# Last stage of a two-layer block on one core, written out step by step instead of looped

## The chip, the cores and the metric
The kernel runs on one core of a Trainium2 chip, as one program from the first load to the last store. The metric is its device time in microseconds (us): 528.04 us before the change (median of 3 runs, 527.6 to 529.25). Engines are called by the profile's names: PE is the matrix engine (PEld its weight loads), DVE the vector engine, ACT the scalar engine, POOL the GpSimd engine, SP the queue that issues most plain DMAs.

## The reference, cut to what matters
x has 8 sequences of 1024 rows of 256 numbers. Two layers follow one another, each adding a product of an attention branch and a gate to x:

```python
xn = _layernorm(x)                       # eps 1e-5
s = _L0_attn_ref(xn, L0_attn_W)          # linear attention
g = _silu(_L0_ffn_ref(xn, gate_w, wg, wu, wd))   # one of 8 experts per row
x = x + s * g
xn = _layernorm(x)
s = _L1_attn_ref(xn, W_qkv, W_out, b_out)        # causal softmax attention in blocks of 128
g = _silu(_L1_ffn_ref(xn, ..., ln_g, ln_b))
x = x + s * g
```

The last feed-forward part sees 8 positions and 16 heads, so each head picks 8 // 16 = 0 rows and adds nothing: what is left of it is a second norm, `(y - mean) * rsqrt(var + eps) * ln_g + ln_b`, over the already normalized rows. The kernel therefore needs two factors per row: 1/sqrt(var + eps) for the attention's input, and the scale of the norm of the normalized row for the gate.

## The kernel before, in words
The program has three stages. The first normalizes the rows, does the linear attention's sums and sorts the rows by expert in DRAM. The second runs the experts on sorted tiles and writes their rows to DRAM (`expert_rows`). The third, `second_layer`, is the one that changes. It handles 64 tiles of 128 rows as 32 units of two tiles; n below is a unit's number.

Each engine has a function `step(n, ...)` and runs it for n in order, so the work is a software pipeline: step n of an engine handles different parts of units near n. The order of every queue is written by hand:
- POOL, step n: `rows_free(n+8)` waits until the indices are there and the buffer is free; `norm_scale(n+2)` makes the row factors with two small operations, `rstd` (L1901, a power of -0.5) and `shift` (L1903); `add_x(n+5)` (L1893) is a DMA that adds x to the unit's rows; `gather(n+8)` (L1883) issues two indirect DMAs that fetch the unit's expert rows. Before `norm_scale` it waits in `rows_scaled(n+5)` for DVE's scaling of that unit's rows.
- DVE, step n: `result(n-2)` (L1809), `index(n+9)` (L1714, converts the next two index columns from float to integer), `norm_stats(n+3)` (L1738), `centre_gate(n+1)` (L1762), `find_moments(n+3)` (L1748), `gate(n-1)` (L1775), `prepare_norm(n+3)` (L1754 to L1756, three operations on two to four numbers per partition), `base_divisor`, `scale_gate(n+1)` (L1769), `maximum(n)` (L1781), `invert_divisor`, `gate_rows(n-1)` (L1803), and last `scale_rows(n+6)` (L1720), which needs the gathered rows.
- ACT, step n: copies of PE's results, `exp(n-1)`, `norm_apply(n+2)` (L1652, writes `xn2nd` and waits for `shift`), `begin_attend`, `tanh(n)`.
- PE, step n: `q(n)` (L1515), `turn(n+1)` (L1528, transposes `xn2nd` and waits for it), `v(n)` (L1537), `turn_probs(n-1)` (L1547), `scores(n)` (L1557), `attend(n-1)` (L1568).
- SP stores the results (L1492).

The first units have an order of their own. For units 0 to 7 x comes by plain loads and DVE adds it (`sum_x`, L1726) right after `scale_rows`; the pair is called `first_rows`. For units 0 to 3 (`NORMED = SLOTS`) the statistics are found at once (`first_norm`). `first_rows(5)` and `first_rows(6)` stand in DVE's step 0, `first_rows(7)` in step 1. On POOL, the factors of units 0 to 3 come in steps -5 to -2; those of unit 4 come in step 2, behind the gathers of units 7, 8 and 9.

The steps are run by `pipeline`: up to n = 7 and from n = 24 on they are written out by Python, and in between a hardware loop (`Fori`) runs twice over eight steps, n = 8 to 23, with addresses worked out from the loop's register. Stage one has no such loop.

Of the kernel before, what the change touches and what calls it, by code (L numbers as in the profile page):

```python
# [14 lines left out]
P = 128  # L15
# [22 lines left out]
def program(nc, x, W, gate_w, wg, wu, wd, W_qkv, W_out, b_out, ln_g, ln_b, out):  # L38
# [16 lines left out]
    with ExitStack() as whole:  # L55
# [16 lines left out]
        z.zinv = sb("zinv", [P, Q_SLOTS, z.UT])  # L72

        z.four = sb("four", [P, 4, z.UT, z.D])
        z.gather_u = sb("gather_u", [P, 8, z.UT], U32)
# [64 lines left out]
def scope(nc, z, ctx, stage):  # L140
# [12 lines left out]
def pipeline(eng, first, step, last, units, slots, tail=1):  # L153


    for n in range(first, slots):
        step(n, n % slots, n // slots)
    with eng.Fori(1, units // slots - tail) as r:
        for i in range(slots):
            step(r * slots + i, i, r)  # L160
    for n in range(units - tail * slots, last + 1):
        step(n, n % slots, n // slots)


def mm3(nc, out, lhs, rhs, first, last, **kw):
# [45 lines left out]
def first_layer(nc, z, W, gate_w, wg, wu, wd):  # L211
# [13 lines left out]
    with ExitStack() as ctx:  # L225
# [698 lines left out]
        def gpsimd(pool):  # L924
# [57 lines left out]
                                    pattern=[[-1, P]], channel_multiplier=1).then_inc(g["consts"], 1)  # L982
            nc.gpsimd.memset(ones_s, 1.0).then_inc(g["consts"], 1)
            nc.gpsimd.iota(ids[:], pattern=[[1, z.SLOTS]], base=0, channel_multiplier=0).then_inc(g["consts"], 1)
            nc.gpsimd.memset(z.neg_half[:], -0.5)
            nc.gpsimd.memset(z.minus_one[:], -1.0)
            nc.gpsimd.memset(xn[:, :, :, D - 1:D], 1.0)
            for e in range(E):
# [15 lines left out]
def experts(nc, z, W_qkv, W_out, b_out, ln_g, ln_b):  # L1004
# [7 lines left out]
    with ExitStack() as ctx:  # L1012
# [287 lines left out]
        def vector(dve):  # L1300
# [23 lines left out]
            def prepare(part):  # L1324

                if part == 0:
                    nc.vector.tensor_tensor(shift_all[:], z.chosen[:], z.moved[:].unsqueeze(1).to_broadcast([P, z.TILES, E]), ALU.mult).then_inc(g["shifts_ready"], 1)
                if part == 1:
                    dve.wait_ge(g["shifts_ready"], 1)
                    nc.vector.tensor_reduce(shift[:], shift_all[:], AX_X, ALU.add).then_inc(g["shift_found"], 1)  # L1330
                if part == 2:
                    dve.wait_ge(g["shift_found"], 1)
                    nc.vector.tensor_tensor(z.place[:, 0:z.TILES], z.place[:, 0:z.TILES], shift[:], ALU.subtract).then_inc(g["shift_found"], 1)
                    nc.vector.tensor_scalar(z.last_one[:], z.ident[:], z.ident[:, P - 1:P], None, ALU.mult).then_inc(z.set_up, 1)
                if part == 3:
                    dve.wait_ge(g["shift_found"], 2)
                    nc.vector.tensor_copy(z.gather_u[:], z.place[:, 0:8 * z.UT].rearrange("p (n t) -> p n t", t=z.UT)).then_inc(z.index_ready, 8)
                if part in (4, 5, 6):
                    of = slice((part - 4) * D, (part - 3) * D)
                    dve.wait_ge(g["weights_loaded"], 16 * 6)  # L1340
                    nc.vector.tensor_tensor(z.w2[:, :, of], z.w2[:, :, of], w2_end[:, of].unsqueeze(1).to_broadcast([P, KD, D]), ALU.subtract).then_inc(g["w2_centred"], 1)
                if part == 7:
                    nc.vector.tensor_scalar(z.lng_half[:], z.lng[:], 0.5, None, ALU.mult).then_inc(z.set_up, 1)
# [68 lines left out]
def second_layer(nc, z):  # L1412
# [7 lines left out]
    UT = 2  # L1420
    UNITS = z.TILES // UT
    SLOTS, TURN = 4, 8
    DIRECT, NORMED = 2 * SLOTS, SLOTS
    MOE_SPACE = 3648
    assert UNITS % TURN == 0 and UT * D <= 512
    with ExitStack() as ctx:
# [35 lines left out]
        g = sems("moe_scaled x_summed stats_done moments_ready var_ready rstd_ready shift_ready xn_ready t_ready t_copied q_ready q_copied "  # L1462
                 "v_ready v_copied s_ready top_ready p_ready pt_ready pt_copied att_ready z_based z_ready "
                 "z_tanh gate_ready total_based inv_ready gated out_ready "
                 "banks_cleared s_begun a_begun folded_ready folded_copied")
# [11 lines left out]

            return not isinstance(n, int) or least <= n < UNITS

        run = lambda eng, first, step, last: pipeline(eng, first, step, last, UNITS, TURN)  # L1480
        at = lambda i, ahead: (i + ahead) % TURN
        turns = lambda n, i, k: (n - i % SLOTS) * (k // SLOTS)

# [224 lines left out]
            run(act, -1, step, UNITS)  # L1708

        def vector(dve):  # L1710
            def index(n, i):

                if there(n):
                    nc.vector.tensor_copy(gather_u[:, i], z.place[:, bass.ds(UT * n, UT)]).then_inc(z.index_ready, 1)  # L1714

            def scale_rows(n, i):

                if there(n):
# [31 lines left out]
            def prepare_norm(n, i):  # L1750

                if there(n):
                    dve.wait_ge(g["moments_ready"], UT * n + UT)
                    nc.vector.tensor_scalar(neg_mean[:, i % SLOTS], moments[:, i % SLOTS, :, 0], -1.0, None, ALU.mult).then_inc(g["var_ready"], 1)  # L1754
                    nc.vector.tensor_scalar(var_eps[:, i % SLOTS, 0], moments[:, i % SLOTS, :, 1], LN_EPS, None, ALU.add).then_inc(g["var_ready"], 1)
                    nc.vector.tensor_scalar(var_eps[:, i % SLOTS, 1], moments[:, i % SLOTS, :, 1], 1.0 + LN_EPS, LN_EPS * LN_EPS, ALU.mult, ALU.add).then_inc(g["var_ready"], 1)  # L1756

            def centre_gate(n, i):
                if there(n):
                    dve.wait_ge(g["shift_ready"], n + 1)  # L1760
                    for t in range(UT):
                        nc.vector.scalar_tensor_tensor(zg[:, i % SLOTS, t, :].unsqueeze(1), one_tile(n, t), neg_mean[:, i % SLOTS, t:t + 1], z.lng_half[:].unsqueeze(1),  # L1762
                                                       ALU.add, ALU.mult).then_inc(g["z_based"], 1)

            def scale_gate(n, i):
                if there(n):
# [57 lines left out]
            def step(n, i, _):  # L1824
# [26 lines left out]
                if isinstance(n, int) and n + 6 < DIRECT:  # L1851
                    if n != -1:
                        first_rows(n + 6, at(i, 6))
                    if n + 6 < NORMED:
                        first_norm(n + 6, at(i, 6))
                else:
                    scale_rows(n + 6, at(i, 6))

            def divisors(p):
# [12 lines left out]
        def gpsimd(pool):  # L1872
            def rows_free(n, i):

                if there(n):
                    pool.wait_ge(z.index_ready, n + 1)
                    if there(n, SLOTS):
                        pool.wait_ge(g["moe_scaled"], n - SLOTS + 1)

            def gather(n, i):  # L1880
                if there(n):
                    for t in range(UT):
                        nc.gpsimd.indirect_dma_start(  # L1883
                            out=moe[:, i % SLOTS, t, :], out_offset=None, in_=z.expert_dram.ap(),
                            in_offset=bass.IndirectOffsetOnAxis(ap=gather_u[:, i, t:t + 1], axis=0)).then_inc(moe_loaded[i % SLOTS], 16)

            def rows_scaled(n, i):
                if there(n):
# [6 lines left out]
            def norm_scale(n, i):  # L1895
                if there(n):
                    if there(n, SLOTS):

                        pool.wait_ge(g["xn_ready"], n - SLOTS + 1)
                    pool.wait_ge(g["var_ready"], 3 * n + 3)  # L1900
                    nc.gpsimd.tensor_tensor(rstd[:, i % SLOTS], var_eps[:, i % SLOTS], z.neg_half[:, 0:2 * UT].rearrange("p (a t) -> p a t", a=2), ALU.pow).then_inc(g["rstd_ready"], 1)  # L1901
                    pool.wait_ge(g["rstd_ready"], n + 1)
                    nc.gpsimd.tensor_tensor(shift[:, i % SLOTS], neg_mean[:, i % SLOTS], rstd[:, i % SLOTS, 0], ALU.mult).then_inc(g["shift_ready"], 1)  # L1903

            def step(n, i, _):
                first = isinstance(n, int) and n + 5 < NORMED
                normed = not first and isinstance(n, int) and n + 2 < NORMED
                direct = isinstance(n, int) and n + 5 < DIRECT
# [8 lines left out]
                if not direct:  # L1917
                    add_x(n + 5, at(i, 5))
                if not first:
                    gather(n + 8, at(i, 8))  # L1920

            for stored in z.stored:
# [27 lines left out]
```

## Time and profile before

| | us |
|---|---|
| time, median of 3 runs | 528.04 |
| time of the profiled execution | 526.61 |
| its span, first to last instruction | 524.9 |
| PE busy | 502.5 (96%) |
| DVE busy | 459.6 (88%) |
| ACT busy | 391.8 (75%) |
| POOL busy | 315.4 (60%) |

The granted clock of PE is 0.996 of full speed. The 3.1 us between the median and the span are 1.7 us around the span in the profiled execution, and 1.4 us by which that execution lay below the median. The busy shares are averages over three stages: DVE and POOL are much busier in the last 200 us (stage three) than these figures say, and a step of that stage has to be read from the timeline.

### The profile page before, as it was taken

What the parts mean: (1) busy time and instruction counts of PE and PEld (TensorE: products, weight loads), DVE (VectorE), ACT (ScalarE), POOL (GpSimd) and SP (SyncE); (2) the same over time, 40 slices, a digit from 0 to 9 for tenths busy, and PEclk for the clock granted to TensorE, in tenths of its full rate; (3) what the DMA queues carried; (4) which work ended last, traced back from release to release, by engine and by line L of the source; (5) the groups of instructions that cost most, each with busy time, mean ns of one, the idle gap of its engine ahead of it and who ended that gap; (6) DMA issues with size and microseconds to landing.
All of it is one profiled execution on the core that took longest, in us unless ns stands there. A gap on an engine that the chain in (4) does not pass through costs nothing.

```text
span 524.9 us, 12534 instructions
## 1 busy us (share of the span) xinstructions
PE 502.5 (96%) x3576; PEld 463.5 (88%) x3577; DVE 459.6 (88%) x1479; ACT 391.8 (75%) x891; POOL 315.4 (60%) x395
## 2 busy tenths in 40 slices
PE   6899999999999999899999999889999999999995
PEld 5899999999999998788999987779888888888894
DVE  6899999999999978589878848899999999999985
ACT  4878878787778863576777746778878887789883
POOL 5468876767777776222122038788888888786410
PEclk9999999999999999999999999999999999999998
DMA  8942322222331115666777454246555665556311
GB/s 224 239 122 93 110 81 81 81 83 87 97 85 67 51 61 194 168 192 191 248 230 230 148 183 151 68 115 139 133 121 125 134 135 128 135 128 120 74 50 61
DMA packets 59409, 67.74 MB, mean 129 GB/s; under 512 B 11864, under 2 KB 53728, under 8 KB 59360
## 3 DMA queue, kind: packets, MB, share of 16 engines
q1 hardware_dynamic: 44960, 39.34, 25.2%
q0 software_dynamic: 14400, 27.80, 21.6%
q8 instruction: 24, 0.39, 0.3%
q14 instruction: 25, 0.20, 0.1%
HBM read 39.85 MB, written 27.26 MB: 128 GB/s over the span
## 4 chain that ended last, share of the span: by engine, by line
PE 63%; DVE 20%; issue 7%; POOL 3%; DMA 2%; ACT 2%; DVEq 1%; SPq 0%; POOLq 0%; ACTq 0%
PE gu_ps L1117 6%; PE v_ps L1537 4%; PE q_ps L1515 3%; PE k_ps L167 3%; PE t_ps L1093 3%; PE y_ps L1136 3%; PE m_ps L167 3%; DVE zg L1762 3%; PE m_ps L169 3%; PE m_ps L168 3%; PE k_ps L168 3%; PE k_ps L169 3%; PE tq_ps L167 3%; PE tq_ps L168 3%; PE tq_ps L169 3%
## 5 line engine op out<-in xcount | busy, mean ns | idle before, releaser
L1883 POOL DMA_INDIRECT four<-expert_rows,gather_u x64 | 70.0, 1094 | 42.5 <-DMA expert_rows<-y 22.3
L948 POOL DMA_INDIRECT sorted_rows<-xn,row_u x64 | 68.0, 1063 | 17.2 <-issue 14.4
L937 POOL TENSOR_TENSOR xn<-xn 128x512 fp32r<-128x512 f32 x32 | 43.2, 1349 | 30.7 <-ACT xn L562 30.6
L1537 PE MATMUL v_ps<-wvo,xt 128*128 128x256 f32 x256 | 60.6, 380 | 0.0
L1515 PE MATMUL q_ps<-xt,wqk 128*128 128x256 f32 x256 | 60.6, 380 | 0.0
L208 POOL DMA_DIRECT2D four<-sorted_rows x36 | 19.4, 540 | 58.7 <-issue 29.4
L1515 PEld LDWEIGHTS q_ps<-xt,wqk 128*128 128x128 f32 x256 | 48.6, 190 | 6.8 <-issue 0.4
L1652 ACT ACTIVATE xn2nd<-res,shift,rstd 128x256 f32<-128x256 f32 (+1 forms) x64 | 34.9, 593 | 23.3 <-POOL shift L1903 23.1
L1537 PEld LDWEIGHTS v_ps<-wvo,xt 128*128 128x128 f32 x256 | 46.4, 191 | 4.9
L1901 POOL TENSOR_TENSOR rstd<-var_eps,neg_half 128x4 f32<-128x4 f32 x32 | 38.6, 1207 | 15.3 <-DVE var_eps L1756 8.2
L1117 PE MATMUL gu_ps<-wgu,xgt 128*128 x288 | 40.2, 283 | 1.2 <-issue 0.9
L167 PE MATMUL tq_ps<-xt,wq 128*128 128x256 f32 x128 | 38.5, 301 | 1.8 <-DVE xt L696 1.8
L552 ACT ACTIVATE xn<-four,shift,rstd 128x255 f32<-128x255 f32 x64 | 34.9, 600 | 6.0 <-POOL shift L931 6.0
L590 ACT ACTIVATE k<-kf 128x512 fp32r<-128x512 f32 x32 | 20.2, 630 | 24.8 <-DVE kf L709 24.8
L167 PE MATMUL k_ps<-wkg,xt 128*128 128x264 f32 x128 | 37.8, 296 | 0.2 <-DVE logit L710 0.2
L1117 PEld LDWEIGHTS gu_ps<-wgu,xgt 128*128 128x128 f32 x288 | 35.0, 192 | 3.0 <-issue 1.9
L167 PE MATMUL m_ps<-k,xn 128*128 128x256 f32 x128 | 36.3, 284 | 0.4 <-DVE k L715 0.4
L168 PE MATMUL k_ps<-wkg,xt 128*128 128x264 f32 x128 | 36.5, 285 | 0.0
L169 PE MATMUL k_ps<-wkg,xt 128*128 128x264 f32 x128 | 36.4, 284 | 0.0
L169 PE MATMUL m_ps<-k,xn 128*128 128x256 f32 x128 | 36.1, 282 | 0.0
L168 PE MATMUL m_ps<-k,xn 128*128 128x256 f32 x128 | 36.1, 282 | 0.0
L1893 POOL DMA_DIRECT2D res<-in_L_attn_x x24 | 31.9, 1328 | 6.7 <-issue 6.7
(262 smaller groups left out, 1780.8 us busy)
## 6 DMA issues: line engine op xcount, KB each, us to landing
expert_rows<-y SPq DMA_DIRECT2D x36, 256.0 KB, 2.8
four<-in_L_attn_x SPq DMA_DIRECT2D x32, 256.0 KB, 2.9
out_rows<-att SPq DMA_DIRECT2D x32, 256.0 KB, 2.3
res<-in_L_attn_x POOLq DMA_DIRECT2D x24, 256.0 KB, 4.5
four<-sorted_rows SPq DMA_DIRECT2D x36, 128.0 KB, 2.3
four<-sorted_rows POOLq DMA_DIRECT2D x36, 128.0 KB, 2.8
wdn<-in_L_ffn_wd SPq DMA_DIRECT2D x2, 512.0 KB, 7.0
sorted_rows<-res SPq DMA_DIRECT2D x8, 128.0 KB, 5.9
```

The source lines that it names most:

```text
L167: nc.tensor.matmul(out, lhs[0], rhs[0], start=first, stop=False, **kw)
L168: nc.tensor.matmul(out, lhs[0], rhs[1], start=False, stop=False, **kw)
L169: return nc.tensor.matmul(out, lhs[1], rhs[0], start=False, stop=last, **kw)
L552: m = nc.scalar.activation(xn[:, i, t, 0:D - 1], xa[:, i % X_SLOTS, t, 0:D - 1], ACT.Identity, bias=shift[:, i % X_SLOTS, t:t + 1], scale= ...
L937: nc.gpsimd.tensor_tensor(xn2[:, s, 1], xn[:, i], xn2[:, s, 0].bitcast(F32), ALU.subtract).then_inc(g["xn_split"], 1)
L948: nc.gpsimd.indirect_dma_start(out=z.sorted_dram.ap(), out_offset=bass.IndirectOffsetOnAxis(ap=row_u[:, i // CU, k:k + 1], axis=0), in_=xn ...
L1117: m = nc.tensor.matmul(gu_ps[:, i % 2, u * 2 * DE:(u + 1) * 2 * DE], xgt[:, i, k, u, :], z.wgu[:, k, bass.ds(e[u], 1), :].rearrange("p a f ...
L1515: m = nc.tensor.matmul(q_ps[:, j, :], wqk[:, k, j * P:(j + 1) * P], xt[:, i % 2, k, :], start=(j == 0 and k == 0), stop=(k == KD - 1), ski ...
L1537: m = nc.tensor.matmul(v_ps[:, t, :], xt[:, i % 2, k, t * P:(t + 1) * P], wvo[:, k, :], start=(t == 0 and k == 0), stop=(k == KD - 1), ski ...
L1652: m = nc.scalar.activation(xn[:, i % SLOTS, t, :].unsqueeze(1), one_tile(n, t), ACT.Identity, bias=shift[:, i % SLOTS, t:t + 1], scale=rst ...
L1883: nc.gpsimd.indirect_dma_start(out=moe[:, i % SLOTS, t, :], out_offset=None, in_=z.expert_dram.ap(), in_offset=bass.IndirectOffsetOnAxis(a ...
L1901: nc.gpsimd.tensor_tensor(rstd[:, i % SLOTS], var_eps[:, i % SLOTS], z.neg_half[:, 0:2 * UT].rearrange("p (a t) -> p a t", a=2), ALU.pow). ...
```

## The change
It touches stage three and what prepares it.
- `pipeline` and its loop go: all steps are written out.
- The indices of all 64 tiles are converted once in stage two (`gather_u` has 64 columns), in place of one conversion of 16 columns there and one per step on DVE. `rows_free` waits for them once.
- DVE's `prepare_norm` becomes one operation: variance plus a pair of constants (eps, and eps squared over 1 + eps). The factor 1/sqrt(1 + eps) that this leaves out goes into `lng_half`. The mean's negation (`neg_mean`) moves to POOL's `norm_scale`, as a third small operation ahead of `rstd`, with waits of its own. `centre_gate` subtracts the mean itself.
- The order at the start: unit 4 gets its `first_norm` in DVE's step 0 (`NORMED = SLOTS + 1`); `first_rows(6)` moves from step 0 to step 1, `first_rows(7)` from step 1 to step 2. On POOL, unit 4's factors come in step -1, right behind `gather(7)` and ahead of `gather(8)` and `gather(9)`; unit 5's come in step 1 ahead of `gather(9)`, where before they came in step 3. Unit 6's come in step 4, as before.

```diff
-    with eng.Fori(1, units // slots - tail) as r:
-        for i in range(slots):
-            step(r * slots + i, i, r)
+        def run(eng, first, step, last):
+            for n in range(first, last + 1):
+                step(n, n % TURN, n // TURN)
...
-                    nc.vector.tensor_copy(z.gather_u[:], z.place[:, 0:8 * z.UT].rearrange("p (n t) -> p n t", t=z.UT)).then_inc(z.index_ready, 8)
+                    nc.vector.tensor_copy(z.gather_u[:], z.place[:, 0:z.TILES]).then_inc(z.index_ready, 1)
...
-    DIRECT, NORMED = 2 * SLOTS, SLOTS
+    DIRECT, NORMED = 2 * SLOTS, SLOTS + 1
...
 (prepare_norm, DVE)
-                    nc.vector.tensor_scalar(neg_mean[:, i % SLOTS], moments[:, i % SLOTS, :, 0], -1.0, None, ALU.mult).then_inc(g["var_ready"], 1)
-                    nc.vector.tensor_scalar(var_eps[:, i % SLOTS, 0], moments[:, i % SLOTS, :, 1], LN_EPS, None, ALU.add).then_inc(g["var_ready"], 1)
-                    nc.vector.tensor_scalar(var_eps[:, i % SLOTS, 1], moments[:, i % SLOTS, :, 1], 1.0 + LN_EPS, LN_EPS * LN_EPS, ALU.mult, ALU.add).then_inc(g["var_ready"], 1)
+                    both = [P, 2, UT]
+                    nc.vector.tensor_tensor(var_eps[:, i % SLOTS], moments[:, i % SLOTS, :, 1].unsqueeze(1).to_broadcast(both),
+                                            z.eps_pair[:].unsqueeze(2).to_broadcast(both), ALU.add).then_inc(g["var_ready"], 1)
...
 (step, DVE)
-                if there(n + 9, TURN):
-                    index(n + 9, at(i, 9))
...
-                if isinstance(n, int) and n == 0:
+                if n == 0:
                     first_rows(n + 5, at(i, 5))
+                    first_norm(n + 4, at(i, 4))
...
+                if 1 <= n <= 2:
+                    first_rows(n + 5, at(i, 5))
+                if n >= 2:
                     scale_rows(n + 6, at(i, 6))
...
 (norm_scale, POOL)
-                    pool.wait_ge(g["var_ready"], 3 * n + 3)
+                    pool.wait_ge(g["moments_ready"], UT * n + UT)
+                    nc.gpsimd.tensor_tensor(neg_mean[:, i % SLOTS], z.zero_pair[:], moments[:, i % SLOTS, :, 0], ALU.subtract).then_inc(g["mean_negated"], 1)
+                    pool.wait_ge(g["var_ready"], n + 1)
                     nc.gpsimd.tensor_tensor(rstd[:, i % SLOTS], var_eps[:, i % SLOTS], z.neg_half[:, 0:2 * UT].rearrange("p (a t) -> p a t", a=2), ALU.pow).then_inc(g["rstd_ready"], 1)
+                    pool.wait_ge(g["mean_negated"], n + 1)
                     pool.wait_ge(g["rstd_ready"], n + 1)
...
 (step, POOL)
                 rows_free(n + 8, at(i, 8))
-                if not direct:
+                if n + 5 >= DIRECT:
                     rows_scaled(n + 5, at(i, 5))
-                if first:
+                if n < 0:
                     gather(n + 8, at(i, 8))
                     norm_scale(n + 5, at(i, 5))
-                elif not normed:
+                if n == 1:
+                    norm_scale(n + 4, at(i, 4))
+                if n >= 4:
                     norm_scale(n + 2, at(i, 2))
```

## Rows read from the trace of the kernel before

**Rows 1.** Busy time in stretches: start:end, length, then per engine busy (xinstructions), clock.

```profile
50.00:100.00 50.00, 50.00 (x436) 49.80 (x435) 46.05 (x159) 40.37 (x77) 38.04 (x43) 1.00 0.29 87
440.00:460.00 20.00, 19.43 (x110) 16.49 (x109) 19.78 (x71) 15.60 (x41) 15.48 (x18) 1.00 0.58 134
```

**Rows 2.** Timeline of PE: start, us, engine, line; starts of q(4), q(6), q(10), q(26), q(31).

```profile
350.17 1.03 PE L1515 MATMUL q_ps<-xt,wqk 128*128 128x256 f32 x4
...
361.92 1.46 PE L1515 MATMUL q_ps<-xt,wqk 128*128 128x256 f32 x6
...
385.41 0.81 PE L1515 MATMUL q_ps<-xt,wqk 128*128 128x256 f32 x3
...
482.55 1.24 PE L1515 MATMUL q_ps<-xt,wqk 128*128 128x256 f32 x5
...
511.91 1.46 PE L1515 MATMUL q_ps<-xt,wqk 128*128 128x256 f32 x6
```

**Rows 3.** Timeline of DVE, small operations of one step in the loop.

```profile
392.83 0.16 DVE L1754 TENSOR_SCALAR neg_mean<-moments 128x2 f32<-128x2 f32 x1
392.90 0.52 DVE L1755 TENSOR_SCALAR var_eps<-moments 128x2 f32<-128x2 f32 x1
...
396.42 0.33 DVE L1714 CAST gather_u<-place 128x2 uint32 x1
396.49 0.75 DVE L1738 BATCH_NORM_STATS2 stats<-res 128x6 f32 x2
```

**Rows 4.** Timeline of POOL, one step (4) ahead of the loop.

```profile
353.88 1.28 POOL L1901 TENSOR_TENSOR rstd<-var_eps,neg_half 128x4 f32<-128x4 f32 x1 [0.31 <-DVE res L1720]
355.24 0.33 POOL L1903 TENSOR_TENSOR shift<-neg_mean,rstd 128x2 f32<-128x2 f32 x1
355.50 1.32 POOL L1893 DMA_DIRECT2D res<-in_L_attn_x  x1
357.13 1.14 POOL L1883 DMA_INDIRECT four<-expert_rows,gather_u  x1 [0.31 <-issue]
358.57 0.98 POOL L1883 DMA_INDIRECT four<-expert_rows,gather_u  x1 [0.30 <-issue]
359.85 1.29 POOL L1901 TENSOR_TENSOR rstd<-var_eps,neg_half 128x4 f32<-128x4 f32 x1 [0.30 <-DVE res L1720]
```

**Rows 5.** Timeline of POOL, one step (21) in the loop: its two ends and add_x.

```profile
457.58 1.31 POOL L1901 TENSOR_TENSOR rstd<-var_eps,neg_half 128x4 f32<-128x4 f32 x1
...
459.61 1.35 POOL L1893 DMA_DIRECT2D res<-in_L_attn_x  x1 [0.44 <-issue]
...
463.63 1.23 POOL L1901 TENSOR_TENSOR rstd<-var_eps,neg_half 128x4 f32<-128x4 f32 x1
```

**Rows 6.** Groups of instructions by line: busy, mean ns, idle before and releaser.

```profile
L1893 POOL DMA_DIRECT2D res<-in_L_attn_x x24 | 31.9, 1328 | 6.7 <-issue 6.7
```

**Rows 7.** Timeline of POOL, the longest such gap.

```profile
447.57 1.35 POOL L1893 DMA_DIRECT2D res<-in_L_attn_x  x1 [1.13 <-issue]
```

**Rows 8.** The line L1903 by itself: min/median/max duration in ns.

```profile
L1903 POOL TENSOR_TENSOR shift<-neg_mean,rstd x32: 189/270/434, 319.8 to 501.3; 128x2 f32<-128x2 f32 x32
```

**Rows 9.** Timeline of DVE in step 0: first_rows(6) waits for its gather.

```profile
334.19 0.69 DVE L1720 TENSOR_TENSOR res<-four,res 128x512 f32<-128x512 f32 x1 [1.85 <-DMA four<-expert_rows,gather_u]
```

**Rows 10.** Timeline of POOL at the start: rstd of units 3, 4, 5.

```profile
332.48 1.05 POOL L1901 TENSOR_TENSOR rstd<-var_eps,neg_half 128x4 f32<-128x4 f32 x1
...
343.15 1.32 POOL L1901 TENSOR_TENSOR rstd<-var_eps,neg_half 128x4 f32<-128x4 f32 x1
...
347.90 1.29 POOL L1901 TENSOR_TENSOR rstd<-var_eps,neg_half 128x4 f32<-128x4 f32 x1 [0.72 <-DVE res L1720]
```

**Rows 11.** The chain that ended last, from rstd(22) to q(22): start, us, what.

```profile
451.57 1.30 POOL rstd L1901
...
454.42 0.66 PE t_ps L1528 x4
...
458.84 1.73 PE q_ps L1515 x8
```

**Rows 12.** The line L1883 by itself: min/median/max duration in ns.

```profile
L1883 POOL DMA_INDIRECT four<-expert_rows,gather_u x64: 942/1068/1511, 308.4 to 474.6; - x64
```

More of the change, by code:

```diff
@@ L74, in program @@
         z.four = sb("four", [P, 4, z.UT, z.D])
-        z.gather_u = sb("gather_u", [P, 8, z.UT], U32)
+        z.gather_u = sb("gather_u", [P, z.TILES], U32)
+        z.eps_pair = sb("eps_pair", [P, 2])
+        z.zero_pair = sb("zero_pair", [P, z.UT])
         z.ident = sb("ident", [P, P])
@@ L150, in scope @@
     return sb, ps, sems
-def pipeline(eng, first, step, last, units, slots, tail=1):
-    for n in range(first, slots):
-        step(n, n % slots, n // slots)
-    with eng.Fori(1, units // slots - tail) as r:
-        for i in range(slots):
-            step(r * slots + i, i, r)
-    for n in range(units - tail * slots, last + 1):
-        step(n, n % slots, n // slots)
 def mm3(nc, out, lhs, rhs, first, last, **kw):
@@ L984, in gpsimd @@
             nc.gpsimd.iota(ids[:], pattern=[[1, z.SLOTS]], base=0, channel_multiplier=0).then_inc(g["consts"], 1)
+            nc.gpsimd.memset(z.zero_pair[:], 0.0)
             nc.gpsimd.memset(z.neg_half[:], -0.5)
+            nc.gpsimd.memset(z.eps_pair[:, 0:1], LN_EPS)
+            nc.gpsimd.memset(z.eps_pair[:, 1:2], LN_EPS * LN_EPS / (1.0 + LN_EPS))
             nc.gpsimd.memset(z.minus_one[:], -1.0)
@@ L1342, in prepare @@
                 if part == 7:
-                    nc.vector.tensor_scalar(z.lng_half[:], z.lng[:], 0.5, None, ALU.mult).then_inc(z.set_up, 1)
+                    nc.vector.tensor_scalar(z.lng_half[:], z.lng[:], 0.5 * (1.0 + LN_EPS) ** -0.5, None, ALU.mult).then_inc(z.set_up, 1)
                 if part == 8:
@@ L1461, in second_layer @@
         value_banks = lambda p: (s2_ps, pa_ps)[(p - END[0]) % 2]
[L1462 removed]
+        g = sems("moe_scaled x_summed stats_done moments_ready mean_negated var_ready rstd_ready shift_ready xn_ready t_ready t_copied q_ready q_copied "
                  "v_ready v_copied s_ready top_ready p_ready pt_ready pt_copied att_ready z_based z_ready "
@@ L1478, in there @@
             return not isinstance(n, int) or least <= n < UNITS
-        run = lambda eng, first, step, last: pipeline(eng, first, step, last, UNITS, TURN)
+        def run(eng, first, step, last):
+            for n in range(first, last + 1):
+                step(n, n % TURN, n // TURN)
         at = lambda i, ahead: (i + ahead) % TURN
@@ L1710, in vector @@
         def vector(dve):
-            def index(n, i):
-                if there(n):
-                    nc.vector.tensor_copy(gather_u[:, i], z.place[:, bass.ds(UT * n, UT)]).then_inc(z.index_ready, 1)
             def scale_rows(n, i):
@@ L1761, in centre_gate @@
                     for t in range(UT):
-                        nc.vector.scalar_tensor_tensor(zg[:, i % SLOTS, t, :].unsqueeze(1), one_tile(n, t), neg_mean[:, i % SLOTS, t:t + 1], z.lng_half[:].unsqueeze(1),
-                                                       ALU.add, ALU.mult).then_inc(g["z_based"], 1)
+                        nc.vector.scalar_tensor_tensor(zg[:, i % SLOTS, t, :].unsqueeze(1), one_tile(n, t), moments[:, i % SLOTS, t, 0:1], z.lng_half[:].unsqueeze(1),
+                                                       ALU.subtract, ALU.mult).then_inc(g["z_based"], 1)
             def scale_gate(n, i):
@@ L1850, in step @@
                     dve.wait_ge(z.rows_ready, UT * UNITS)
[L1851 to L1854, printed above, removed]
+                if n < -1:
+                    first_rows(n + 6, at(i, 6))
+                    if n < -2:
                         first_norm(n + 6, at(i, 6))
-                else:
+                if 1 <= n <= 2:
+                    first_rows(n + 5, at(i, 5))
+                if n >= 2:
                     scale_rows(n + 6, at(i, 6))
@@ L1875, in rows_free @@
                 if there(n):
-                    pool.wait_ge(z.index_ready, n + 1)
+                    if n == 0:
+                        pool.wait_ge(z.index_ready, 1)
                     if there(n, SLOTS):
@@ L1884, in gather @@
                             out=moe[:, i % SLOTS, t, :], out_offset=None, in_=z.expert_dram.ap(),
-                            in_offset=bass.IndirectOffsetOnAxis(ap=gather_u[:, i, t:t + 1], axis=0)).then_inc(moe_loaded[i % SLOTS], 16)
+                            in_offset=bass.IndirectOffsetOnAxis(ap=gather_u[:, UT * n + t:UT * n + t + 1], axis=0)).then_inc(moe_loaded[i % SLOTS], 16)
             def rows_scaled(n, i):
@@ L1905, in step @@
             def step(n, i, _):
-                first = isinstance(n, int) and n + 5 < NORMED
-                normed = not first and isinstance(n, int) and n + 2 < NORMED
-                direct = isinstance(n, int) and n + 5 < DIRECT
                 rows_free(n + 8, at(i, 8))
-                if not direct:
+                if n + 5 >= DIRECT:
                     rows_scaled(n + 5, at(i, 5))
-                if first:
+                if n < 0:
                     gather(n + 8, at(i, 8))
                     norm_scale(n + 5, at(i, 5))
-                elif not normed:
+                if n == 1:
+                    norm_scale(n + 4, at(i, 4))
+                if n >= 4:
                     norm_scale(n + 2, at(i, 2))
-                if not direct:
+                if n + 5 >= DIRECT:
                     add_x(n + 5, at(i, 5))
-                if not first:
+                if n >= 0:
                     gather(n + 8, at(i, 8))
```

## The prediction

> **What bounds the kernel now.** I read the busy time by stretches first, to see where the change can act. Stage three runs from about 323 us to the end, and in its middle PE and DVE are both nearly full: of 20 us PE is busy 19.43 and DVE 19.78 [rows 1]. A sum of busy time can't say which of them sets the pace, so I went to the timeline and took the start of `q(n)` for every unit. q(26) to q(31) takes 511.91 - 482.55 = 29.36 us, 5.87 a unit, and so does q(6) to q(10) (23.49, four units) [rows 2]. In these two stretches PE's matmuls follow one another without a wait, so 5.87 is PE's own floor. From q(10) to q(26) it takes 97.14 us, 6.07 a unit. So the middle loses 16 x 0.20 = 3.2 us against the floor, and that is the most that a faster DVE or POOL can return there.
>
> What takes the 0.20? The ordinary DVE step there is 5.97 us without a gap, 0.10 over the floor. For its parts the reader must look at starts, not durations: L1754 to L1755 and L1714 to L1738 are 0.07 us apart although each is listed with 0.16 to 0.5 us, since small operations overlap on DVE [rows 3]. The other half of the loss sits in a few longer steps, where POOL is late or an engine passes an end of the loop. Ahead of the loop its step is 359.85 - 353.88 = 5.97 us, of which 0.30 is a wait for DVE's `scale_rows`, so 5.67 of its own [rows 4]. Inside the loop one reads 463.63 - 457.58 = 6.05 with no wait for DVE at all, and 0.44 of it is an "issue" gap ahead of `add_x` that the same instruction doesn't have in straight code [rows 4, 5]. There are 16 such gaps, 6.7 us in all [rows 6], and the longest is 1.13 [rows 7]. POOL's `shift` releases `norm_apply` on ACT, and that releases PE's `turn`. So POOL counts although it is called 60% busy.
>
> **DVE's small operations.** A step loses the conversion, the negation and one of two variance operations: 3 x 0.07 = 0.21 us by the distance of starts [rows 3]. The upper bound by listed durations would be 0.16 to 0.5 each, but the next operation starts 0.07 later whatever they say. The new variance operation has two inputs and a broadcast; it could cost 0.07 (like its neighbours) to 0.2. I take 0.07. DVE's step goes from 5.97 to 5.76, below PE's floor. What comes late next is PE at 5.87, so only 0.10 of the 0.21 counts. The one conversion of 64 columns in stage two replaces one of 16 columns; I take nothing for it either way, it is one small operation among hundreds.
>
> **Straight code.** POOL's gap ahead of `add_x` goes: 0.42 on average [rows 6], and the overlap of 0.07 that straight code shows (L1893 starts at 355.50, `shift` ends at 355.57) comes back [rows 4]. DVE and POOL also lose three passages into, around and out of the loop. More instructions have to be fetched instead of reused. Stage one is straight code with the same matmul density, and there PE is busy 50.00 of 50 us [rows 1], so I take nothing for fetching. The Trainium skill, page "Runtime: NRT & Kernel Launch", section "Instruction fetch mechanics", says that straight code is streamed ahead and that a taken branch outside the window held costs a fetch. This trace agrees about the straight half; it changes nothing in the sum.
>
> **The negation on POOL.** This is the edit that speaks against the change. It adds one operation per unit ahead of `rstd`, and behind it are queued `rstd`, `shift`, `add_x` and both gathers; ACT's `norm_apply` and through it PE wait for them. The nearest row is `shift`, of the same shape: 0.19 at least, 0.27 median, 0.43 at most [rows 8], and 0.08 until the next starts (355.16 to 355.24) [rows 4]. So 0.27 to 0.51 a step. From the step in the loop: 6.05 - 0.44 - 0.07 = 5.54, and with the negation 5.81 to 6.05. From the step ahead of the loop, with its wait taken out: 5.67, and with the negation 5.94 to 6.18. POOL will be behind DVE (see the start), as in the loop, so the first pair is nearer; with the median duration it gives 5.54 + 0.35 = 5.89. I take 5.90 a unit, just over PE's 5.87.
>
> A row first: `rstd` in rows 4 starts while DVE adds two SBUF tiles (L1809) and takes 1.28, where the one in a quiet spot takes 1.05 [rows 4, 10]. The Trainium skill, page "SBUF — State Buffer", section "Who interferes with whom" and the section on the two sides ahead of it, says that a DVE operation with two SBUF inputs and a GpSimd operation that reads SBUF exclude each other for the whole instruction. By that rule the negation, which comes right behind `scale_rows` and so into `result`'s addition, would always be held to that addition's end: the slower rival below. The trace shows 0.23 of delay where the rule would give the rest of an addition of 0.69 (as the one in rows 9), so it agrees only in direction.
>
> **The order of the first units.** Now DVE's step 0 waits 1.85 us for the gather of unit 6 [rows 9], which delays `maximum(1)`, and unit 4's factors wait on POOL behind six gathers: from 332.48 to 343.15 [rows 10]. Both waits go. I put q(4) at about 347, 3.3 us before its 350.17 [rows 2]. But POOL works nearly without pause from its first gather on, and the new order leaves all its work in. From the start to `rstd(6)` at 353.88 it waits only 0.72 and 0.31 [rows 4, 10], so without waits `rstd(6)` could be at 352.85. Seven negations (units 0 to 6) come on top, each 0.27 to 0.35: 1.9 to 2.4. That makes 354.7 to 355.3. From `rstd(22)` to `q(22)`, where POOL is what PE waits for, it takes 458.84 - 451.57 = 7.3 us [rows 11]. So q(6) can't come before 362.0 to 362.6, and it is at 361.92 now [rows 2]. The lead of 3.3 us at unit 4 is spent waiting for unit 6: the start brings -0.2 us (from -0.7 to, with small stretches gone, +0.5).
>
> **The sum.** From q(6) to q(26) it takes 482.55 - 361.92 = 120.63 us now; at 5.90 it is 118.0, a gain of 2.6. After q(26) POOL has no gathers left and PE runs at its floor in both. With the start's -0.2 the gain is 2.4 us. The profiled execution took 526.61 us and would take 524.2. The median of the runs is 1.43 higher, 528.04, and what I forecast is a median: 528.04 - 2.4 = 525.6 us.
>
> **Rivals.**
> - PE at its floor and the lead kept. If POOL's gathers are cheaper without DVE's two-input additions beside them, POOL no longer holds unit 6 and the 3.3 us of the start stay, with 20 x 5.87 = 117.4, 3.2 less, behind it: 528.04 - 6.5 = 521.5. For it: one gather takes anything between 0.94 and 1.51 [rows 12]. Against it: six stretches of up to half a microsecond would have to vanish.
> - POOL takes DVE's place at DVE's pace. If its step is 6.0, 20 units take 120.0, and with -0.2 the gain is 0.4: 527.6. For it: the upper end of the first pair of bounds, 6.05. Against it: DVE's two-input additions come at another time then.
> - POOL becomes a worse bound. The place is the negation behind `rows_scaled`, the price 0.51 a step on the 5.67 of rows 4: 6.18 x 20 = 123.6, and with -0.2 it is 3.2 slower: 531.2. It decides from 120.63 / 20 = 6.03 us a POOL step on. For it: the step that waits for `scale_rows` begins exactly in DVE's next addition. Against it: a POOL that is late no longer begins there.
> - The change doesn't do what it says, because straight code meets fetch stalls on one engine or another where the loop had none: within a microsecond of 528. Only the 1.13 gap [rows 7], inside the loop, has no cause that I can see.
>
> **Chances.** Forecast 0.55, lead kept 0.10, DVE's pace 0.20, worse bound 0.10, fetch stalls 0.05. A measurement of this kernel tells 0.3%, 1.6 us, from no change. The forecast reaches 5.94 a step before it falls under that, so a tenth of its weight counts as no change. Faster by over 0.3%: 0.50 + 0.10 + 0.05 of the third = 0.65. Slower by over 0.3%: the worse bound, 0.10. Within: 0.25. The forecast's own range, at steps of 5.87 to 5.94, is 524.3 to 526.6, the start's +0.5 and -0.7 beside it. For 8 in 10 I go down part of the way to the kept lead and up past the DVE's pace: 522.6 to 528.4.
>
> **What would show it.** In the changed kernel: no "issue" gap ahead of L1893; DVE's step with waits of about 0.1 us in it; q(4) near 347 but q(6) near 362, with PE waiting for `xn2nd` at unit 6; 20 units from q(6) to q(26) in 118 us; the negation listed at 0.19 to 0.43. The prediction is wrong if q(6) comes under 360, if POOL's step reads 6.0 or more, or if PE shows gaps that no engine releases.

## The result: slower by 1.3%

| | before | changed |
|---|---|---|
| median of 4 runs, us | 528.54 | 535.20 |
| lowest to highest | 527.6 to 529.25 | 532.74 to 537.31 |
| profiled execution, its span | 526.61, 524.9 | 537.31, 535.7 |

The ratio is 1.0129, with a 95% interval of 1.0098 to 1.0159. I had forecast 525.6 us; the sign was wrong too. What happened is the third rival, POOL as a worse bound, at more than its price and for reasons that were not in it.

The same starts of q(n) as in [rows 2], from PE's timeline of the changed kernel (q(4), q(6), q(26), q(31)):

```profile
350.40 0.38 PE L1511 MATMUL q_ps<-xt,wqk 128*128 128x256 f32 x1
...
367.86 0.38 PE L1511 MATMUL q_ps<-xt,wqk 128*128 128x256 f32 x1
...
493.27 0.38 PE L1511 MATMUL q_ps<-xt,wqk 128*128 128x256 f32 x1
...
522.64 0.38 PE L1511 MATMUL q_ps<-xt,wqk 128*128 128x256 f32 x1
```

The span grew by 10.8 us, more than the medians. POOL's first gather starts at 311.51, 3.06 us later than before (308.45). That is ahead of everything that was changed but a few small operations; PE's granted clock reads 0.97 in 0 to 50 us and in 200 to 250 us of this execution, and 1.00 before; the kernel `neg_dve` below reads 0.97 in the same stretches and has its first gather at 312.89, and at 309.86 when traced once more, so one kernel's executions differ by as much, and these 3 us can't be put down to the change. From the first gather to q(6) it takes 56.35 us, before 53.47: 2.9 lost. From q(6) to q(26) it takes 125.41, before 120.63: 4.8 lost, 6.27 a unit where I had put 5.90. From q(26) to q(31) nothing changes (29.37). So 7.7 us belong to stage three in this execution, the slowest of the four.

POOL's timeline of the changed kernel, one step of the middle, to be held against [rows 4] and [rows 5]:

```profile
422.72 1.10 POOL L1895 TENSOR_TENSOR rstd<-var_eps,neg_half 128x4 f32<-128x4 f32 x1
423.96 0.20 POOL L1898 TENSOR_TENSOR shift<-neg_mean,rstd 128x2 f32<-128x2 f32 x1
424.41 1.33 POOL L1885 DMA_DIRECT2D res<-in_L_attn_x  x1 [0.25 <-issue]
426.05 1.09 POOL L1875 DMA_INDIRECT four<-expert_rows,gather_u  x1 [0.31 <-issue]
427.44 1.50 POOL L1875 DMA_INDIRECT four<-expert_rows,gather_u  x1 [0.30 <-issue]
428.94 0.23 POOL L1893 TENSOR_TENSOR neg_mean<-zero_pair,moments 128x2 f32<-128x2 f32 x1
429.09 1.08 POOL L1895 TENSOR_TENSOR rstd<-var_eps,neg_half 128x4 f32<-128x4 f32 x1
```

No row of it waits for another engine ("issue" is idle time for which the profile shows no wait): POOL is full, and a step is 429.09 - 422.72 = 6.37 us (the next one is 6.26). From `rstd(10)` to `rstd(24)` POOL's step is 6.35 us on average, before it was 6.13. The negation itself takes 0.15 from start to start here, 0.20 on average. What the reader should see is the rest. The gap ahead of `add_x` (L1885) is still 0.25, where straight code before had an overlap of 0.07 [rows 4]; 0.14 us pass between `rstd` and `shift`, not 0.08; and the second gather takes 1.50, not 0.98. By line (busy, mean ns, idle before), against [rows 6]:

```profile
L1885 POOL DMA_DIRECT2D res<-in_L_attn_x x24 | 32.0, 1332 | 6.2 <-issue 5.7 <-DVE moments L1739 0.5
```

The gaps of 6.7 us that were to go with the loop are 5.7 us in straight code. What runs beside the gather of 1.50 stands in DVE's timeline:

```profile
427.43 0.66 DVE L1766 SCALAR_TENSOR_TENSOR zg<-th,zg 128x512 f32<-128x512 f32 x1
428.00 0.15 DVE L1746 TENSOR_TENSOR var_eps<-moments,eps_pair 128x4 f32<-128x4 f32 x1
```

The gather starts 0.01 us after a DVE operation on two SBUF tiles, whose successor starts 0.57 later; it takes 0.52 longer than its usual 0.98. In this trace the second gather is longer the more of such an operation is left when it starts: 1.18 with 0.24 left, 1.25 with 0.32, 1.41 with 0.47.

PE pays through `xn2nd`. By waits of PE's weight loads (total us, times, longest):

```profile
PEld t_ps L1524 <- ACT xn2nd L1648: 15.1, 19, 3.4
```

The longest is the one at unit 6, which I had expected. PE's timeline there, and the busy time and granted clock (third column from the end) of the stretches around it:

```profile
362.00 0.66 PE L1524 MATMUL t_ps<-ident,xn2nd 128*128 128x128 f32 x4 [3.04 <-ACT xn2nd L1648]
362.49 2.73 PE L1533 MATMUL v_ps<-wvo,xt 128*128 128x256 f32 x8
```

```profile
355.00:360.00 5.00, 3.92 (x22) 3.27 (x22) 4.93 (x16) 1.64 (x4) 4.39 (x5) 1.00 0.80 167
360.00:365.00 5.00, 3.00 (x12) 2.46 (x13) 4.96 (x15) 3.79 (x10) 3.98 (x5) 0.84 0.48 99
365.00:370.00 5.00, 5.00 (x27) 4.62 (x26) 2.60 (x7) 3.52 (x8) 4.10 (x6) 0.82 0.47 95
370.00:375.00 5.00, 5.00 (x30) 4.51 (x29) 4.83 (x17) 4.40 (x13) 4.30 (x5) 1.00 0.56 136
```

After the wait of 3.0 us PE runs part of the next stretch at the lower of its two levels, 1.2 GHz: `v` takes 2.73 us (1.89 in `neg_dve2` below, where the clock reads 1.00), and from `turn(6)` to q(6) 5.86 us pass where [rows 11] have 4.42. That is 1.4 of the 2.9 us lost up to q(6).

### The profile page after: what moved, and what is told of

Its sections match the earlier page's. It is cut to its first block, busy times and chain, and to the rows that moved or that the text cites. A ratio compares the mean times of both kernels' runs of the same rounds, so it can differ in the third digit from the quotient of the medians.

```text
span 535.7 us, 12150 instructions
## 1 busy us (share of the span) xinstructions
PE 509.6 (95%) x3576; PEld 467.3 (87%) x3577; DVE 454.7 (85%) x1390; ACT 392.3 (73%) x891; POOL 327.7 (61%) x430
## 4 chain that ended last, share of the span: by engine, by line
PE 60%; POOL 18%; DVE 10%; issue 7%; ACT 2%; DMA 2%; SPq 0%; POOLq 0%; DVEq 0%; ACTq 0%
POOL four L1875 9%; PE gu_ps L1110 6%; POOL rstd L1895 4%; PE k_ps L157 3%; PE v_ps L1533 3%; POOL res L1885 3%; PE t_ps L1086 3%; PE m_ps L157 3%; PE m_ps L159 3%; PE y_ps L1129 3%; PE m_ps L158 3%; PE tq_ps L157 3%; PE k_ps L158 3%; PE k_ps L159 3%; PE tq_ps L158 3%
## 5 line engine op out<-in xcount | busy, mean ns | idle before, releaser
L1875 POOL DMA_INDIRECT four<-expert_rows,gather_u x64 | 74.1, 1157 | 42.1 <-DMA expert_rows<-y 22.3
L1648 ACT ACTIVATE xn2nd<-res,shift,rstd 128x256 f32<-128x256 f32 x64 | 35.0, 596 | 32.2 <-POOL shift L1898 32.2
L157 PE MATMUL tq_ps<-xt,wq 128*128 128x256 f32 x128 | 38.7, 302 | 2.0 <-DVE xt L686 2.0
L1895 POOL TENSOR_TENSOR rstd<-var_eps,neg_half 128x4 f32<-128x4 f32 x32 | 36.9, 1154 | 0.2
L159 PE MATMUL tq_ps<-xt,wq 128*128 128x256 f32 x128 | 36.1, 282 | 0.0
```

The source lines that it names most:

```text
L157: nc.tensor.matmul(out, lhs[0], rhs[0], start=first, stop=False, **kw)
L159: return nc.tensor.matmul(out, lhs[1], rhs[0], start=False, stop=last, **kw)
L1648: m = nc.scalar.activation(xn[:, i % SLOTS, t, :].unsqueeze(1), one_tile(n, t), ACT.Identity, bias=shift[:, i % SLOTS, t:t + 1], scale=rst ...
L1875: nc.gpsimd.indirect_dma_start(out=moe[:, i % SLOTS, t, :], out_offset=None, in_=z.expert_dram.ap(), in_offset=bass.IndirectOffsetOnAxis(a ...
```

## The experiments

Theory N: the negation on POOL, with its waits, is the cost and the rest of the change is a gain. Rivals: T, straight code is dearer; O, the new order of the first units costs. Four kernels, each with one part undone or done alone.

**Straight code alone**, on the kernel before.

```diff
-        run = lambda eng, first, step, last: pipeline(eng, first, step, last, UNITS, TURN)
+        def run(eng, first, step, last):
+            for n in range(first, last + 1):
+                step(n, n % TURN, n // TURN)
```

> The kernel before with its loop written out and nothing else changed (the index conversion per step stays on DVE, the negation too). Theory N (the negation on POOL lengthens a POOL step that was already as long as PE's, and nothing else in the change costs anything): POOL's step stays under 5.97 us, DVE at 5.97 sets the pace for units 6 to 26, time 525 to 528 us. Rival T (straight code itself is dearer, by fetching or by issue gaps that stay): 531 us or more, and POOL's step at 6.2 or more though it does no negation.

Measured: 525.6 us, ratio to before 0.9946 (0.9924 to 0.9969). From POOL's timeline in the middle:

```profile
397.39 1.29 POOL L1903 TENSOR_TENSOR rstd<-var_eps,neg_half 128x4 f32<-128x4 f32 x1 [0.30 <-DVE res L1722]
398.76 0.32 POOL L1905 TENSOR_TENSOR shift<-neg_mean,rstd 128x2 f32<-128x2 f32 x1
399.02 1.34 POOL L1895 DMA_DIRECT2D res<-in_L_attn_x  x1
...
403.36 1.28 POOL L1903 TENSOR_TENSOR rstd<-var_eps,neg_half 128x4 f32<-128x4 f32 x1 [0.30 <-DVE res L1722]
```

The gap ahead of `add_x` is gone, POOL waits 0.30 us for DVE, and q(6) to q(26) takes 119.25 us, 5.96 a unit: DVE's pace. As N has it; T falls.

**The negation back on DVE** (`neg_dve`), on the changed kernel.

```diff
 (prepare_norm, DVE)
+                    nc.vector.tensor_scalar(neg_mean[:, i % SLOTS], moments[:, i % SLOTS, :, 0], -1.0, None, ALU.mult).then_inc(g["var_ready"], 1)
 (norm_scale, POOL)
-                    pool.wait_ge(g["moments_ready"], UT * n + UT)
-                    nc.gpsimd.tensor_tensor(neg_mean[:, i % SLOTS], z.zero_pair[:], ...).then_inc(g["mean_negated"], 1)
-                    pool.wait_ge(g["var_ready"], n + 1)
-                    pool.wait_ge(g["var_ready"], n + 1)
+                    pool.wait_ge(g["var_ready"], 2 * n + 2)
...
-                    pool.wait_ge(g["mean_negated"], n + 1)
                     pool.wait_ge(g["rstd_ready"], n + 1)
```

> The changed kernel with the negation back on DVE as one small operation (0.07 us by the distance of starts) and one wait less on POOL; all else as changed. Theory N: the POOL step falls from 6.31 us to under 5.9, PE's floor of 5.87 sets the pace from unit 6 to 26, time 523 to 527 us. Rival T (straight code) and rival O (the new order of the first units costs the time, through a long wait of PE at unit 6): 531 us or more, with the POOL step near 6.2 under T and the wait at unit 6 still 3 us under O.

Measured: 521.58 us, 0.9878 (0.9856 to 0.9901), 1.4 us below the range of N, and q(6) to q(26) takes 117.47 us: PE's floor of 5.87 in every one of the 20 units. The new order of the first units is still in, so O falls too. The same kernel measured once more gave 523.9 us, 0.9927 (below): the two intervals do not meet, so 2 us between kernels measured on different occasions tell nothing.

**The old order of the first units**, on the changed kernel.

```diff
-    DIRECT, NORMED = 2 * SLOTS, SLOTS + 1
+    DIRECT, NORMED = 2 * SLOTS, SLOTS
...
 (and first_norm(4), first_rows(6), first_rows(7), norm_scale(4), norm_scale(5) where they stood before)
```

> The changed kernel with the order of before for the first rows, norms and gathers; negation on POOL, straight code. Theory N: a step from unit 6 to 26 stays at about 6.3 us and the time within 2 us of the changed kernel's, 533 to 536 us. Rival O: the time falls to 528 to 530 us, since PE's wait at unit 6 and the fall of its clock behind it go.

Measured: 535.13 us, 1.0133 (1.011 to 1.0156), with 6.33 us a unit (126.68 for 20). As N has it; O falls.

**The negation alone on POOL**, on the kernel before, loop and order kept; the lines are those of the change.

> The kernel before, loop and order kept, with the negation alone moved to POOL (with its two waits; DVE keeps both variance operations). Theory N: inside the loop the POOL step grows from 6.03 by 0.3 to 0.5 us, so units 8 to 24 take 6.3 to 6.5 us each, time 533 to 537 us. Rival T (it is the straight code and not the negation): 528 to 530 us.

Measured: 536.47 us, 1.0154 (1.0126 to 1.0182), 127.37 us for 20 units, 6.37 a unit. The negation on POOL, with its two waits, gives the whole loss by itself. In the loop little of it is the gap ahead of `add_x`: from `rstd(10)` to `rstd(24)` POOL's step goes from 6.13 to 6.49 us, and the gap from 0.41 to 0.46.

That left open what about it is so dear. An operation of 0.20 us from its start to the next doesn't make 0.52 a step (POOL's 6.35 against 5.83 in the kernel with the negation on DVE, where nothing is lost). Theory W: its waits. Theory V: the operation and what it meets on DVE.

**Negation on POOL, two waits fewer.**

```diff
-                    pool.wait_ge(g["moments_ready"], UT * n + UT)
-                    nc.gpsimd.tensor_tensor(neg_mean[:, i % SLOTS], z.zero_pair[:], ...).then_inc(g["mean_negated"], 1)
                     pool.wait_ge(g["var_ready"], n + 1)
+                    nc.gpsimd.tensor_tensor(neg_mean[:, i % SLOTS], z.zero_pair[:], ...).then_inc(g["rstd_ready"], 1)
...
-                    pool.wait_ge(g["mean_negated"], n + 1)
-                    pool.wait_ge(g["rstd_ready"], n + 1)
+                    pool.wait_ge(g["rstd_ready"], 2 * n + 2)
```

> The changed kernel with the negation still on POOL but two waits fewer a step: one wait for the variance ahead of it, and one wait for both of POOL's own results ahead of shift, where the changed kernel has two and two. Theory W (the waits are the dearer half: they hold POOL's queue, so that the gap from shift to add_x is 0.25 us where it is -0.06 without the negation): the gap goes back near -0.06, the step falls from 6.3 to 5.9 or 6.0, time 523 to 528 us. Theory V (the operation itself and its meeting with DVE's two-input operations are what costs): the step stays at 6.2 or more, time 531 us or more.

Measured: 531.65 us, 1.0082 (1.0053 to 1.011). From POOL's timeline, two steps:

```profile
407.52 0.40 POOL L1893 TENSOR_TENSOR neg_mean<-zero_pair,moments 128x2 f32<-128x2 f32 x1
407.88 1.30 POOL L1894 TENSOR_TENSOR rstd<-var_eps,neg_half 128x4 f32<-128x4 f32 x1
409.26 0.20 POOL L1896 TENSOR_TENSOR shift<-neg_mean,rstd 128x2 f32<-128x2 f32 x1
409.39 1.33 POOL L1885 DMA_DIRECT2D res<-in_L_attn_x  x1
411.02 1.38 POOL L1875 DMA_INDIRECT four<-expert_rows,gather_u  x1 [0.30 <-issue]
412.70 1.18 POOL L1875 DMA_INDIRECT four<-expert_rows,gather_u  x1 [0.30 <-issue]
413.88 0.47 POOL L1893 TENSOR_TENSOR neg_mean<-zero_pair,moments 128x2 f32<-128x2 f32 x1
```

The gap has gone, as W says. But the time lies in V's range and 3.7 us above W's, and a unit takes 6.16 us (123.21 for 20), nearer to V's 6.2 than to W's 5.9 to 6.0. So the waits are not the dearer half: without them the negation on POOL still loses most of it. POOL's steps are in turn 5.87 and 6.43, since the negation now starts beside DVE operations and takes 0.40 to 0.47, and in every other step both gathers are held as well.

**Two spare waits on POOL, negation on DVE**, both on semaphores passed long before.

```diff
+                    pool.wait_ge(g["moments_ready"], UT * n + UT)
                     pool.wait_ge(g["var_ready"], 2 * n + 2)
...
+                    pool.wait_ge(g["stats_done"], UT * n + UT)
                     pool.wait_ge(g["rstd_ready"], n + 1)
```

> The kernel with the negation on DVE and two waits more on POOL a step, both long satisfied: one ahead of rstd, one ahead of shift. No operation is added. Theory W: the gap from shift to add_x grows from -0.06 to 0.2 or more and the gap ahead of shift from 0.08 to 0.14, the step from 5.83 to about 6.0, time 523 to 527 us (521.6 without them). Theory V: the step stays at 5.83 and the time at 521 to 522.5.

Measured: 529.46 us, 1.0025 (1.0004 to 1.0047), 6.06 a unit. The mechanism is as W has it (gap 0.25, 0.14 ahead of `shift`), but the time is 2.5 us above its range. V, by which waits cost nothing, falls. Two waits that never wait cost more than the whole gain.

**Negation twice on POOL**, the second into a tile that nobody reads, without a wait.

```diff
+                    nc.gpsimd.tensor_tensor(spare[:, i % SLOTS], z.zero_pair[:], moments[:, i % SLOTS, :, 0], ALU.subtract)
```

> The changed kernel with a second negation on POOL a step, into a tile that nobody reads, without a wait of its own. By the operation alone, 0.15 us from start to start as in the changed kernel's quiet steps, the step goes from 6.3 to 6.45, 20 units cost 3 us, time 537 to 539 us. Theory V, that each further operation also meets one more of DVE's: 6.6 to 6.8, time 541 us or more. Theory W: the first figure.

Measured: 537.35 us, 1.02 (1.0163 to 1.0236), within the lower expectation, but a unit takes only 6.33, not 6.45 (126.69 for 20; POOL's own step is 6.42 on average, with one negation 6.35): the second negation takes 0.15 from start to start, and the second gather is held less (at most 1.41, not 1.52). Part of what is added to POOL is taken off the time that it is held.

**Which of the two spare waits**, each alone, on the kernel with the negation on DVE; that kernel itself was measured beside them (523.9 us, below). First the one between `rstd` and `shift`.

> The kernel with the negation on DVE and one of the two spare waits: the one between rstd and shift, behind which add_x is queued. Theory S (what counts is a second wait in POOL's queue between rstd and add_x, since it is passed only when rstd is done): the gap from shift to add_x is 0.25 us here, the step 5.9 to 6.0, time near that with both waits (529.5), at least 525. Rival A (any spare wait costs the same, half of it each): half the gap, about 0.1, time 524 to 526.

Measured: 530.61 us, 1.0061 (1.0042 to 1.0081), 6.08 a unit, somewhat more than the 5.9 to 6.0 expected. From POOL's timeline:

```profile
399.94 1.38 POOL L1894 TENSOR_TENSOR rstd<-var_eps,neg_half 128x4 f32<-128x4 f32 x1
401.47 0.19 POOL L1897 TENSOR_TENSOR shift<-neg_mean,rstd 128x2 f32<-128x2 f32 x1
401.92 1.35 POOL L1886 DMA_DIRECT2D res<-in_L_attn_x  x1 [0.25 <-issue]
```

One step later the gap is 0.60 and near unit 21 it is 1.03; nearly all others are 0.25. Then the wait ahead of `rstd`.

> The kernel with the negation on DVE and the other spare wait, ahead of rstd. Theory S: the gap from shift to add_x stays at -0.06, the step at 5.83 and the time at 521 to 523 us. Rival A: gap about 0.1, time 524 to 526.

Measured: 524.02 us, 0.9943 (0.992 to 0.9965), 5.87 a unit, the same as without it (523.9, below). The time is 1 us above S's range and in rival A's, since both ranges were set from the 521.6 of the earlier occasion; gap (-0.06) and step (5.83) are S's, not A's. So S holds: a wait ahead of `rstd` costs nothing that these runs can tell, and one between `rstd` and `shift` costs 6.7 us. That it costs because it is passed only when `rstd` is done is the theory's reason; no run separates it from others.

**The order once more**: negation on DVE with the old order, and then new (`neg_dve2`) and old order side by side. The first run of the old order:

> The kernel with the negation on DVE and the old order of the first rows, norms and gathers. If the new order has a value of its own once POOL is relieved, this takes 1 to 2.5 us longer than the kernel with the new order (521.6): 522.5 to 524 us, with q(3) and q(4) late as before. If the order is worth nothing, as the prediction had it (POOL's work up to unit 6 decides), 521.3 to 522.3 us.

Measured: 522.25 us, 0.9897 (0.9871 to 0.9923), by the range an order that is worth nothing.

> The kernel with the negation on DVE once more, beside the same with the old order, since the two differed by less than their runs do (521.6 and 522.3). By its trace the new order brings q(31) 1.2 us nearer to the first rstd: 521 to 522.5 us, 0.5 to 1.5 us under the other. If the order is worth nothing the two are within 0.5 us.

> The kernel with the negation on DVE and the old order of the first units once more: 522 to 523.5 us, 0.5 to 1.5 us over the new order if that is worth something, the same within 0.5 us if not.

Measured: 523.9 us, 0.9927 (0.9907 to 0.9946), 1.4 above the range, and 523.4 us, 0.993 (0.9907 to 0.9954). They are 0.5 us apart, and the new order is not the faster. The order is worth nothing that these runs can tell, and the 1.2 us that I read from one pair of traces were not the order's. From q(6) to q(26) both take 117.47 us. From POOL's timeline of the new order:

```profile
402.12 1.35 POOL L1876 DMA_INDIRECT four<-expert_rows,gather_u  x1 [0.30 <-issue]
403.48 1.25 POOL L1894 TENSOR_TENSOR rstd<-var_eps,neg_half 128x4 f32<-128x4 f32 x1
404.80 0.20 POOL L1896 TENSOR_TENSOR shift<-neg_mean,rstd 128x2 f32<-128x2 f32 x1
404.94 1.32 POOL L1886 DMA_DIRECT2D res<-in_L_attn_x  x1
```

And one row of the old (`neg_dve_old`):

```profile
400.52 1.37 POOL L1892 TENSOR_TENSOR rstd<-var_eps,neg_half 128x4 f32<-128x4 f32 x1 [0.19 <-DVE res L1711]
```

POOL's step is 5.83 us in both. With the old order it waits 0.2 us of that for DVE; with the new one it does not, but its second gather takes 1.35 where it takes 0.98 with the old. So 5.83 is DVE's pace there, and POOL needs less.

## Why the prediction was wrong

- **What bounds the kernel.** Right. PE's floor of 5.87, DVE at 5.97 above it and a POOL of about 6 that counts in spite of its 60%: with the gap gone a unit falls to DVE's 5.96, and with the negation on DVE, where both engines are relieved, all 20 units fall to 5.87.
- **DVE's small operations.** Right in kind and size. With straight code alone a unit takes 5.96; with the conversion and a variance operation gone too, it takes 5.87 and DVE, at 5.83 a step, no longer sets the pace. DVE's step falls by the two distances of 0.07 that went. 20 x 0.09 = 1.8 us; I had 0.10 a unit.
- **Straight code.** Right by itself: 0.9946, and the gap of 0.42 goes. Wrong in the sum. The step of the prediction that failed is the 5.90 us a unit, and it failed by two terms; this is the first, a term put at nothing: "POOL's gap ahead of `add_x` goes". It goes only if nothing else holds POOL's queue between `rstd` and `add_x`. The change puts a second wait there (for `mean_negated`), and the gap is 0.25 instead of -0.07. I had named what is queued behind the negation and left its waits unpriced. That wait alone, on the kernel with the negation on DVE, costs 121.58 - 117.47 = 4.1 us over the 20 units and 6.7 us by medians.
- **The negation on POOL.** This is the second term. I had 0.27 to 0.51 a step, 0.35 taken, on 5.54 of POOL's own, 5.90 in all. The run with two waits fewer has the gap gone, as my sum had it, and still takes 6.16 a unit: 0.26 of the 0.37 by which the changed kernel's 6.27 passes 5.90. What the price left out is when the operations behind it start: there the negation begins beside DVE's operations and takes 0.40 to 0.47, and in every other step both gathers take 0.2 to 0.3 longer. The two prices do not add up: over 20 units the negation without the extra waits costs 5.7 us (123.21 - 117.47), the wait alone 4.1, both together 7.9 (125.41 - 117.47). So both are shown to cost, and the share of each in the loss stays open. By parts, POOL's step of 6.35 has 0.33 of gap, 0.06 from `rstd` to `shift` and 0.20 of negation more than the 5.83 with the negation on DVE, and 0.14 less in `rstd`. That 5.54 + 0.35 + 0.32 + 0.06 gives 6.27, which is 125.41 / 20, is luck. Twenty steps at 0.37 over the forecast are 7.4 of the 9.6 us between forecast and median.
- **The first units.** I had said that POOL's work would eat the 3.3 us that q(4) gains, and put q(6) 0.2 later. q(4) does come 2.8 us sooner after the first gather (38.9 against 41.7) and q(6) 2.9 us later, 1.4 of it PE's lower clock after its wait, and PE does wait for `xn2nd` at unit 6. But the same kernel traced twice (`neg_dve`, `neg_dve2`) has 51.15 and 53.89 us from first gather to q(6). The four kernels that have the negation and its waits on POOL have 55.3 to 57.4, all others 51.2 to 55.0: the direction is shown, the 2.9 us of one trace are not.
- **The chances.** The worse bound had 0.10, with a decision point of 6.03 a step. The price that I gave it (6.18) was below what came, and its condition, a negation right behind `scale_rows`, wasn't even met. I reasoned from two POOL steps that differ in their gap (0.44 and -0.07) without asking what makes the gap; that question would have raised its chance.
- **Two readings.** I read the 0.23 us by which `rstd` is longer in [rows 4] against "the rest of an addition of 0.69". The addition had begun before `rstd` (353.88), and DVE's next operation starts at 354.17:

```profile
353.57 0.69 DVE L1809 TENSOR_TENSOR att<-att,res 128x512 f32<-128x512 f32 x1
354.17 0.17 DVE L1714 CAST gather_u<-place 128x2 uint32<-128x2 f32 x1
```

  Only 0.29 us of it were left, so the delay is nearly the whole rest and not a third of it. And the upper end of the forecast's own range comes to 526.9 us by its terms (5.94 a step and the start's -0.7), not 526.6, which changes nothing.

Not settled: from one traced execution to the next the part ahead of the first gather differs by 4.4 us (308.45 to 312.89), so single traces can't tell what 1 us of the start is worth. The run with the wait between `rstd` and `shift` is 6.7 us slower by medians, and its trace 5.0 us longer in span; 1.5 of the other 1.7 are that the traced execution without the wait lay 1.3 above its median (525.24) and the one with it 0.2 below (530.45). And every kernel that has gaps ahead of `add_x`, the one before among them, has one of 1.0 to 1.2 us near unit 21 (1.13 in [rows 7]), while no kernel without such gaps has it (straight code alone, the negation on DVE, the one with two waits fewer, the spare wait ahead of `rstd`). So it goes with the gap; what makes it long there no run shows.

## What to carry to other kernels

An engine that is busy 60% over the kernel can be full in one stage; add up one of its steps, gaps included, before anything is moved to it. Price its waits too: on POOL one wait that never waits, set between a result and a DMA that is queued behind it, cost 6.7 us over 32 units. The operation that was moved had cost DVE 0.07 us a unit; on POOL, even without the extra waits, it cost 5.7 us over 20 units, held beside DVE's operations together with what is queued behind it. Where two results of one engine are needed, one semaphore for both saves a wait: here the gap of 0.25 us went with it.

## What the runs showed of the hardware that I had not expected

- A satisfied wait on POOL is not free, and its place decides. In straight code, between `rstd` and `shift` it brings the gap ahead of the next DMA from -0.06 to 0.25 us and that ahead of `shift` from 0.08 to 0.14; ahead of `rstd` it changes neither.
- A POOL operation on SBUF tiles or an indirect DMA that starts beside a DVE operation on two SBUF tiles is held for about the rest of it: 0.52 for a gather that starts with 0.56 left; 0.3 for the gather at 411.02 (1.38, its usual is 1.08), started with 0.35 of an addition left; 0.23 for `rstd` in [rows 4] with 0.29 left. `add_x`, a direct DMA, is not: at 418.15 in the changed kernel it starts with 0.59 of `scale_rows` left and takes its usual 1.34. In the prediction I read the 0.23 as a partial hold and said that the Trainium skill's page "SBUF — State Buffer", section "Who interferes with whom", agreed only in direction. These rows agree with its exclusive lock in size as well. The same section infers that a `tensor_tensor` on DVE does not hold a DMA's descriptor work; that fits `add_x`, but not the gather at 411.02.
- PE's clock fell after a wait of 3.0 us in the changed kernel (0.84 and 0.82 in two stretches of 5 us), so that a late step there cost about half as much again. The kernel with two negations has the same: a wait of 3.2 us, then 0.66 over 5 us.
